# Four result tiles in place of two, and the last sequence's averaging products ahead of an output product

## The chip, the cores and the metric

The kernel runs on one core of one Trainium2 chip. The metric is device time in microseconds (us) of one execution; lower is better. Names of engines: PE is TensorE (PEld its weight loads), DVE is VectorE, ACT is ScalarE, POOL is GpSimd, SP is SyncE, which here only issues DMAs.

## The reference

A block over eight sequences of 512 rows and 128 channels, all in float32. After a layer norm, one branch is a recurrent attention (a running weighted mean over time), the other is one expert of a feed-forward layer with a second layer norm and a SiLU; their product is added to the input.

```python
xn = layernorm(x)                                   # x: (8, 512, 128)
shifted = pad(xn, one row of zeros ahead)[:, :-1]
k, v, r = (mix(xn, shifted, m) @ W for m, W in ((mk, Wk), (mv, Wv), (mr, Wr)))
wkv = scan over t of (e1 * num + e2 * v) / (e1 * den + e2)
s = (sigmoid(r) * wkv) @ Wo
z = xn + relu(xn @ w1 + b1) @ w2 + b2               # expert 0 alone has a weight, 1
g = silu((z - mean(z)) * rsqrt(var(z) + 1e-5) * gamma + beta)
out = x + s * g
```

## The kernel before

Each sequence is one tile of 128 channels (partitions) by 512 time steps, so a step of the work on one sequence is mostly one instruction. The order of the work is written out by hand: `PROGRAM` (line 27) holds one list of steps for each engine, and `run` (line 280) issues them. A token `s:5` is step `s` of sequence 5; `var.a:7` is the first half (256 time steps) of step `var` of sequence 7. Only the first and the last sequence have halves. Each engine takes its list strictly in its order, and waits at a step for all that the step names by `after`.

The last part of the program is what matters here. For one sequence it goes like this:

- `gated` (DVE, line 849) is the gated attention result, in `gated[b % 2]`. It reads the bank of `r`, which is free after it.
- `s` (PE, line 661) is the output product with `Wo`, into a bank. A float32 product of 512 columns is two matmuls in the trace.
- `sq` (ACT, line 523) squares z; `var` (PE, line 668) is the averaging product: it multiplies the squares by a matrix of 1/128, which gives the variance of each column. `ln_var` and `rstd2` (ACT, lines 529 and 536) make the inverse root of it from a logarithm and an exponential, `zn` (DVE, line 858) the normed z, and `silu` (ACT, line 584) the gate g. Between `rstd2` and `silu` stands a load of another activation table (line 455), between `sq` and `ln_var` one too (line 452).
- `prod` (DVE, line 866) multiplies g with the bank of `s`; `back` (PE, line 689) transposes it to rows, four matmuls of 128 columns; `res` (DVE, line 875) adds the input and writes the result tile `res[b % 2]`; `store` (line 307) sends the tile out, 256 KB, from SP's queue. The last half, `res.b:7`, goes out from ACT's queue (line 593).

Two kinds of resource tie the steps together besides the data:

- Eight PSUM banks. `BANKS` (line 78) lists for each bank who holds it in turn, and `FREED_BY` (line 90) which step frees it. `bank_free` (line 247) makes a PE step wait for that. The bank of `var.a:7` was held by `r:6`, so the step waits for `gated:6`; the bank of `var.b:7` was held by `v:7`, so it waits for `wkv:7`; that of `s:5` was held by `k:7`, so it waits for `adev:7`.
- Result tiles. `res` of sequence b writes a tile that the store of sequence b - 2 reads, so `add_input` (line 868) waits until that store has landed (`stored`, two semaphores).

`prod:5` waits for `s:5`, and `gated:7` reuses the tile of `gated:5`, which `s:5` reads.

Of the kernel before, what the change touches and what calls it, by code (L numbers as in the profile page):

```python
# [7 lines left out]
ALU = mybir.AluOpType  # L8
# [4 lines left out]
WARM_UP = 8  # L13
KEEP_WARM_BETWEEN = 1
KEEP_WARM = 4
LN_EXP_TABLES = "natural_log_exp_and_others"
SILU_TABLES = "silu_and_others"

# [13 lines left out]
        up1:3 k:3 z2:3 z0:3 z1:3 var:2 s:0 z3:3 up3:4 k:4 T:5 up0:4 up2:4 var:3 s:1 back:0 v:3 up1:4  # L32
        back:1 z3:4 z0:4 v:4 s:2 up2:5 z1:4 z2:4 r:3 T:6 up1:5 r:4 z2:5 k:5 var:4 up3:5 up0:5 T:7
        up1:6 v:5 up0:6 up2:6 s:3 up3:6 r:5 k:6 z1:5 z0:5 z3:5 k:7 z3:6 var:5 z1:6 z0:6 z2:6 v:6
        back:2 var:6 up1:7 up2:7 up3:7 v:7 s:4 z2:7 up0:7 r:6 r:7 z1:7 z3:7 z0:7 back:3 s:5 var.b:7
        var.a:7 back:4 s:6 s.b:7 back:5 s.a:7 back:6 back.a:7 back.b:7
    """,
    "act": """
        ln_exp ve.a:0 rs.a:0 neg_td ve.b:0 rs.b:0 w1_hi xT.a:0 xT.b:0 wo ve:1 rs:1 hid0:0 xT:1
# [7 lines left out]
        ln_var:4 hid3:5 rstd2:4 xT:7 hid0:5 e_new:5 e_keep:5 hid0:6 v_sb:5 hid2:6 ln_den:5 silu_set  # L47
        th_g:5 silu:4 hid3:6 th_r:5 th_a:5 sq:5 ln_exp e_new:6 e_keep:6 ln_var:5 rstd2:5 e_keep:7
        sq:6 ln_den:6 e_new:7 v_sb:6 ln_var:6 rstd2:6 ln_den:7 hid2:7 silu_set th_g:6 v_sb:7 th_a:6
        th_g:7 silu:5 hid0:7 th_a:7 th_r:7 silu:6 th_r:6 sq.a:7 sq.b:7 ln_exp ln_var.b:7 ln_var.a:7  # L50
        rstd2.b:7 rstd2.a:7 silu_set silu.a:7 silu.b:7
    """,
    "dve": """
        bn.a:0 aggr1.a:0 bn.b:0 aggr1.b:0 norm1.a:0 norm1.b:0 cols bn:1 aggr1:1 d:0 w2_sum inv:0
# [5 lines left out]
        dev:4 gated:3 adev:4 wkv:4 mx:5 gated:4 gap:5 inv:6 zn:4 hid1:6 ink:6 den:5 prod:3 inr:6  # L60
        rel:5 ink:7 mx:6 dev:5 gap:6 adev:5 mx:7 gap:7 wkv:5 den:6 gated:5 zn:5 inv:7 res:2 den:7
        hid1:7 rel:6 inr:7 zn:6 rel:7 prod:4 hid3:7 dev:6 adev:6 dev:7 wkv:6 adev:7 wkv:7 gated:6
        res:3 prod:5 gated:7 res:4 zn.b:7 zn.a:7 prod:6 res:5 prod.a:7 prod.b:7 res:6 res.a:7
        res.b:7
    """,
    "pool": """
# [62 lines left out]
def build_block(nc, x, vectors, squares, w1, w2, out):  # L129
    B, T, H = x.shape  # L130
    P = 128
    NT = T // P
# [5 lines left out]
    out_rows = out.rearrange("b (j p) c -> b p j c", p=P)  # L138
# [8 lines left out]
    with ExitStack() as ctx:  # L147
        def sb(name, *shape, dt=FP32):
            return ctx.enter_context(nc.sbuf_tensor(name, list(shape), dt))

        def pair(name, *shape, dt=FP32):
            return [sb(f"{name}_{n}", *shape, dt=dt) for n in range(2)]
# [25 lines left out]
        ve1 = sb("ve1", P, B * NT)  # L178
        rstd1 = sb("rstd1", P, B * NT)
        xn = pair("xn", P, NT, P)  # L180
        res = pair("res", P, NT, P)


        xT = pair("xT", P, 1 + T)
# [12 lines left out]
        th_g = pair("th_g", P, T)  # L197
# [6 lines left out]
        gated = pair("gated", P, T)  # L204
        hid = pair("hid", P, NF, T)
        sq = pair("sq", P, T)
        ln_var = pair("ln_var", P, T)
        rstd2 = pair("rstd2", P, T)
        zn = pair("zn", P, T)
        g = pair("g", P, T)  # L210
        prod = pair("prod", P, T)
# [3 lines left out]
        def ps(name, b, half=""):  # L215
            return banks[bank_of[name, half if (name, half, b) in bank_of else "", b]]

        def sem(name):
            return ctx.enter_context(nc.semaphore(name))
# [5 lines left out]
                 "w2_sum", "w2_mean", "w2"]}  # L225
        done = {(engine, name): sem(f"{name}_by_{engine}")
                for engine, name in dict.fromkeys((signal[token][0], token[0]) for token in signal if token[2] is not None)}
        stored = [sem(f"stored_{n}") for n in range(2)]
        EDGES = 11
        LAST = B - 1  # L230
        CHUNKS = [f"z{f}" for f in range(NF)]

        def after(eng, step, b, half=""):
            if b < 0 or (b == 0 and step in NOT_FOR_FIRST):
                return
            if (step, half, b) in signal:
                engine, count = signal[step, half, b]
            elif half:
                engine, count = signal[step, "", b]
            else:  # L240
                engine, count = max(signal[step, h, b] for h in "ab")
            eng.wait_ge(done[engine, step], count)
# [13 lines left out]
        def chunks_of(b):  # L256

            return [name for name, _, i in tokens("pe") if name in CHUNKS and i == b]
# [4 lines left out]
        def tiles(half):  # L263
            return {"": slice(0, NT), "a": HALVES[0], "b": HALVES[1]}[half]
# [8 lines left out]
        def first_on(engine, step):  # L273
            return [b for name, _, b in tokens(engine) if name == step][0]
# [23 lines left out]
        def load_half(eng, h):  # L298
            tiles = HALVES[h]
            eng.dma_start(x_sb[:, tiles.start * P:tiles.stop * P].rearrange("p (j c) -> p j c", c=P),  # L300
                          x_rows[0][:, tiles, :]).then_inc(got[f"x0_{h}"], 16)

        def load(eng, b):
            eng.dma_start(x_sb[:, b * T:(b + 1) * T].rearrange("p (j c) -> p j c", c=P),
                          x_rows[b]).then_inc(got[f"x{b}"], 16)

        def store(eng, b, half=""):
            after(eng, "res", b, half)
            eng.dma_start(out_rows[b][:, tiles(half), :], res[b % 2][:, tiles(half), :]).then_inc(stored[b % 2], 16)

        block = ctx.enter_context(nc.Block())

        @block.sync
        def _(sp):
            load_half(sp, 0)
            sp.dma_start(w1_in[:, :], w1).then_inc(got["w1"], 16)
            sp.dma_start(w_in[:, :, :], squares).then_inc(got["squares"], 16)
            load(sp, 1)
            sp.dma_start(w2_in[:, :, :], w2.rearrange("(f p) c -> p f c", p=P)).then_inc(got["w2"], 16)
            for b in range(2, B):  # L320
                load(sp, b)
            for b in range(LAST):
                store(sp, b)
            store(sp, LAST, "a")
            sp.wait_ge(stored[0], 16 * (B // 2))
            sp.wait_ge(stored[1], 16 * (B // 2 + 1))

        @block.gpsimd
        def _(pool):
# [117 lines left out]
        def _(act):  # L447
# [3 lines left out]
            def ln_exp_tables():  # L451
                act.preload_act_table_set(LN_EXP_TABLES)  # L452

# [137 lines left out]
            steps.update({f"hid{f}": hidden(f) for f in range(NF)})  # L591
            run("act", steps)
            store(act, LAST, "b")

        @block.tensor
        def _(pe):
            def keep_warm(count):
                for _ in range(count):
                    pe.matmul(banks[WARM_BANK][:, 0:P], ident[:, :], ident[:, :], start=True, stop=True)  # L599
# [8 lines left out]
            def transposes(b, half=""):  # L608
# [9 lines left out]
                elif b == 0:  # L618
                    keep_warm(KEEP_WARM)

# [80 lines left out]
        def _(dve):  # L701
# [166 lines left out]
            def add_input(b, half=""):  # L868
                t = tiles(half)
                after(dve, "back", b, half)  # L870
                if b >= 2:
                    dve.wait_ge(stored[b % 2], 16 * (b // 2))
                rows = x_sb[:, b * T:(b + 1) * T].rearrange("p (j c) -> p j c", c=P)
                summed = ps("back", b, half)[:, :].rearrange("p (j c) -> p j c", c=P)
                dve.tensor_tensor(res[b % 2][:, t, :], summed[:, t, :], rows[:, t, :], ALU.add).then_inc(done["dve", "res"], 1)

            steps = {"bn": stats, "aggr1": aggregate, "norm1": normalise, "d": step_of_x, "xT_lo": low_part, "dv": value_steps,
                     "cols": small_columns, "w2_sum": w2_row_sums, "mx": running_max, "gap": exponents,
                     "den": denominator, "rel": relative, "dev": deviation,
                     "wkv": mixed_values, "gated": gate, "zn": scale, "prod": multiply, "res": add_input,  # L880
                     "adev": weighted}
            steps.update({"in" + name: mix(name) for name in "kvr"})
# [35 lines left out]
```

## Time and profile before

| What | Value |
|---|---|
| Time, median of 3 runs | 111.28 us (110.7 to 111.68) |
| Time of the profiled execution | 111.6 us |
| Its span (first to last instruction) | 109.8 us |
| PE busy | 100.7 us, 92% |
| DVE busy | 99.3 us, 90% |
| ACT busy | 93.4 us, 85% |
| POOL busy | 67.0 us, 61% |
| DMA | 5.09 MB, mean 46 GB/s |

The span is a part of the time: the profiled execution has 1.8 us around it. Times inside the span count from its start. Busy shares are means over the whole span; they don't say which engine sets the end. In a row of the timeline, two numbers stand first: the start, and the length in us. Rows of a merged group (x2, x4) give the whole group's length. The records of matmuls overlap, since they are pipelined, so their cadence is read from the starts.

### The profile page before, as it was taken

The numbers are of one execution on the slowest core, as the hardware profiler recorded it, in microseconds if no ns is written. First come the engines' busy times: TensorE is split into PE (matmuls) and PEld (weight loads), VectorE is DVE, ScalarE is ACT, GpSimd is POOL, SyncE is SP. The second block draws the span as 40 slices with busy tenths as digits, with TensorE's granted clock in tenths as the row PEclk, the third lists the DMA queues.
The fourth block names the chain that finished last, engine by engine and source line by source line (L and its number), as shares of the span: only waits on it lengthen the run. The fifth ranks groups of instructions, "written<-read, shape, count | busy, mean of one in ns | idle before, by whom it ended". The sixth has DMA issues, their size and how long they took to land.

```text
span 109.8 us, 1625 instructions
## 1 busy us (share of the span) xinstructions
PE 100.7 (92%) x340; PEld 57.8 (53%) x340; DVE 99.3 (90%) x204; ACT 93.4 (85%) x155; POOL 67.0 (61%) x102
## 2 busy tenths in 40 slices
PE   4999989999699999999999999999989999999720
PEld 4998546654346465436574554754424565435410
DVE  1789799999889999998999899999999999999941
ACT  3550888999979999999999999999998999998800
POOL 3059699986838599999699669594645033700000
PEclk9999999999999999999999999999999999999995
DMA  2999300000000000000005000000000020001463
GB/s 90 279 314 291 83 0 0 0 6 0 3 0 3 0 0 0 0 0 0 0 15 178 1 6 0 0 0 3 0 0 0 0 96 0 9 0 57 134 191 99
DMA packets 9450, 5.09 MB, mean 46 GB/s; under 512 B 480, under 2 KB 9184, under 8 KB 9440
## 3 DMA queue, kind: packets, MB, share of 16 engines
q1 hardware_dynamic: 8752, 4.72, 15.3%
q10 hardware_dynamic: 688, 0.27, 0.9%
q14 instruction: 7, 0.06, 0.2%
q8 instruction: 3, 0.05, 0.2%
HBM read 2.89 MB, written 2.10 MB: 45 GB/s over the span
## 4 chain that ended last, share of the span: by engine, by line
PE 56%; issue 15%; POOL 13%; ACT 6%; DVE 5%; DMA 2%; DVEq 1%; POOLq 0%; ACTq 0%
PE bank L630 11%; PE bank L680 10%; PE bank L599 5%; PE bank L661 5%; PE bank L668 5%; PE bank L651 4%; POOL xn L359 4%; PE bank L653 4%; PE bank L652 4%; PE bank L613 3%; PE bank L643 3%; POOL xT_lo L381 2%; DMA block_out<-res 2%; POOL gap_max L415 2%; PE bank L689 2%
## 5 line engine op out<-in xcount | busy, mean ns | idle before, releaser
L680 PE MATMUL bank<-hid,w_c 128*128 128x512 f32 x64 | 30.8, 593 | 0.3 <-ACT hid L514 0.3
L630 PE MATMUL bank<-mixed,w_in 128*128 128x512 f32 x48 | 24.0, 599 | 1.1 <-POOL mixed L399 1.1
L514 ACT ACTIVATE hid<-bank,vec 128x512 f32<-128x512 f32 x28 | 18.8, 684 | 3.6 <-PE bank L643 2.9
L680 PEld LDWEIGHTS bank<-hid,w_c 128*128 128x128 f32 x64 | 11.9, 189 | 12.6 <-issue 11.6
L786 DVE SCALAR_TENSOR_TENSOR mixed<-step_x,vec,bank 128x511 f32<-128x511 f32 x24 | 17.2, 735 | 0.8 <-POOL step_x L390 0.8
L651 PE MATMUL bank<-xT_hi,w_hi 128*128 128x512 f32 x28 | 15.7, 560 | 0.0
L359 POOL TENSOR_SCALAR xn<-x_sb,neg_mean,rstd 128x128 f32<-128x128 f32 x28 | 14.1, 521 | 0.1
L630 PEld LDWEIGHTS bank<-mixed,w_in 128*128 128x128 f32 x48 | 8.4, 189 | 9.3 <-issue 8.2
L423 POOL TENSOR_TENSOR dv<-v_sb 128x512 f32<-128x512 f32 x8 | 8.9, 1108 | 6.1 <-ACT v_sb L567 6.1
L825 DVE TENSOR_TENSOR_SCAN dev<-keep,dv 128x512 f32<-128x512 f32 x8 | 11.5, 1435 | 0.6 <-issue 0.3
L653 PE MATMUL bank<-xT_lo,w_hi 128*128 128x512 f32 x28 | 11.1, 395 | 0.0
L652 PE MATMUL bank<-xT_hi,w_lo 128*128 128x512 f32 x28 | 11.0, 394 | 0.0
L795 DVE TENSOR_TENSOR_SCAN mx<-td,bank 128x512 f32<-128x512 f32 x8 | 9.7, 1210 | 0.7 <-PE bank L630 0.7
L430 POOL TENSOR_SCALAR keep<-th_g 128x512 f32<-128x512 f32 x8 | 5.8, 723 | 6.3 <-ACT th_g L573 6.2
L810 DVE TENSOR_TENSOR_SCAN den<-e_keep,bank 128x512 f32<-128x512 f32 x8 | 9.6, 1208 | 0.0
L452 ACT ACT_TABLE_LOAD x6 | 7.7, 1283 | 1.9 <-issue 1.8
L710 DVE BATCH_NORM_STATS2 stats<-x_sb 128x6 f32<-128x128 f32 x32 | 6.9, 278 | 2.6 <-DMA x_sb<-x 2.6
L381 POOL TENSOR_TENSOR xT_lo<-xT,xT_hi 128x512 fp32r<-128x512 f32 x7 | 8.9, 1267 | 0.3
L668 PE MATMUL bank<-sq,averager 128*128 128x512 f32 (+1 forms) x18 | 8.3, 557 | 0.5 <-DVE adev L833 0.5
L661 PE MATMUL bank<-gated,wo_half 128*128 128x512 f32 (+1 forms) x18 | 8.3, 553 | 0.0
L651 PEld LDWEIGHTS bank<-xT_hi,w_hi 128*128 128x128 f32 x28 | 5.3, 188 | 5.5 <-issue 2.1
L407 POOL TENSOR_SCALAR gap_min<-gap,td 128x512 f32<-128x512 f32 x8 | 5.5, 688 | 4.2 <-DVE gap L803 4.0
(72 smaller groups left out, 209.9 us busy)
## 6 DMA issues: line engine op xcount, KB each, us to landing
x_sb<-x SPq DMA_DIRECT2D x7, 256.0 KB, 5.4
block_out<-res SPq DMA_DIRECT2D x7, 256.0 KB, 2.3
w_in<-w SPq DMA_DIRECT2D x2, 256.0 KB, 4.0
w_in<-squares SPq DMA_DIRECT2D x1, 256.0 KB, 3.9
x_sb<-x ACTq DMA_DIRECT2D x1, 128.0 KB, 2.8
x_sb<-x SPq DMA_DIRECT2D x1, 128.0 KB, 2.5
block_out<-res SPq DMA_DIRECT2D x1, 128.0 KB, 1.9
block_out<-res ACTq DMA_DIRECT2D x1, 128.0 KB, 2.0
```

What stands on the lines that cost most here:

```text
L359: ins = pool.tensor_scalar(xn[n][:, j, :], x_tile(b, j), neg_mean1[:, i:i + 1], rstd1[:, i:i + 1], ALU.add, ALU.mult)
L381: pool.tensor_tensor(xT_lo[n][:, :], xT[n][:, 1:], xT_hi[n][:, :].bitcast(FP32), ALU.subtract).then_inc(done["pool", "xT_lo"], 1)
L514: act.activation(hid[b % 2][:, f, :], ps(f"up{f}", b)[:, :], ACT.Relu, bias=vec[:, B1_COLUMN + f:B1_COLUMN + f + 1]).then_inc(done["act", ...
L630: pe.matmul(ps(name, b)[:, :], w_in[:, which, :], mixed[b % 2][:, which, :], start=True, stop=True).then_inc(done["pe", name], 1)
L651: pe.matmul(dst, hi, xT_hi[n][:, :], start=True, stop=False)
L652: pe.matmul(dst, lo, xT_hi[n][:, :], start=False, stop=False)
L653: pe.matmul(dst, hi, xT_lo[n][:, :], start=False, stop=True).then_inc(done["pe", f"up{f}"], 1)
L661: pe.matmul(ps("s", b, half)[:, c], wo_half[:, :], gated[b % 2][:, c], start=True, stop=True).then_inc(done["pe", "s"], 1)
L668: pe.matmul(ps("var", b, half)[:, c], averager[:, :], sq[b % 2][:, c], start=True, stop=True).then_inc(done["pe", "var"], 1)
L680: pe.matmul(ps("z", b)[:, :], w2_c[:, f, :], hid[b % 2][:, f, :], start=False, stop=chunks_of(b)[-1] == f"z{f}", skip_group_check=True).th ...
L786: dve.scalar_tensor_tensor(mixed[n][:, which, 1:], step_x[n][:, 1:], vec[:, which:which + 1], ps("z", b)[:, 0:T - 1], ALU.mult, ALU.add).t ...
L825: dve.tensor_tensor_scan(dev[n][:, :], keep[n][:, 0:T], dv[n][:, :], 0.0, ALU.mult, ALU.add).then_inc(done["dve", "dev"], 1)
```

## The change

`res` has four tiles in place of two, and there are four `stored` semaphores. So `res` of sequence b waits for the store of sequence b - 4, and `res:0` to `res:3` wait for none. In the program of PE, the averaging products of sequence 7 stand ahead of `s:5` in place of behind it, and half a ahead of half b. ACT's `ln_var` and `rstd2` and DVE's `zn` of sequence 7 also take half a first. `BANKS` and `FREED_BY` stay as they are. All else stays.

```diff
@@ PROGRAM "pe"
-        back:2 var:6 up1:7 up2:7 up3:7 v:7 s:4 z2:7 up0:7 r:6 r:7 z1:7 z3:7 z0:7 back:3 s:5 var.b:7
-        var.a:7 back:4 s:6 s.b:7 back:5 s.a:7 back:6 back.a:7 back.b:7
+        back:2 var:6 up1:7 up2:7 up3:7 v:7 s:4 z2:7 up0:7 r:6 r:7 z1:7 z3:7 z0:7 back:3 var.a:7
+        var.b:7 s:5 back:4 s:6 s.b:7 back:5 s.a:7 back:6 back.a:7 back.b:7
@@ PROGRAM "act"
-        th_g:7 silu:5 hid0:7 th_a:7 th_r:7 silu:6 th_r:6 sq.a:7 sq.b:7 ln_exp ln_var.b:7 ln_var.a:7
-        rstd2.b:7 rstd2.a:7 silu_set silu.a:7 silu.b:7
+        th_g:7 silu:5 hid0:7 th_a:7 th_r:7 silu:6 th_r:6 sq.a:7 sq.b:7 ln_exp ln_var.a:7 ln_var.b:7
+        rstd2.a:7 rstd2.b:7 silu_set silu.a:7 silu.b:7
@@ PROGRAM "dve"
-        res:3 prod:5 gated:7 res:4 zn.b:7 zn.a:7 prod:6 res:5 prod.a:7 prod.b:7 res:6 res.a:7
+        res:3 prod:5 gated:7 res:4 zn.a:7 zn.b:7 prod:6 res:5 prod.a:7 prod.b:7 res:6 res.a:7
@@ tiles and semaphores
+RES = 4
-        res = pair("res", P, NT, P)
+        res = [sb(f"res_{n}", P, NT, P) for n in range(RES)]
-        stored = [sem(f"stored_{n}") for n in range(2)]
+        stored = [sem(f"stored_{n}") for n in range(RES)]
@@ store
-            eng.dma_start(out_rows[b][:, tiles(half), :], res[b % 2][:, tiles(half), :]).then_inc(stored[b % 2], 16)
+            eng.dma_start(out_rows[b][:, tiles(half), :], res[b % RES][:, tiles(half), :]).then_inc(stored[b % RES], 16)
@@ the end of SP's program
-            sp.wait_ge(stored[0], 16 * (B // 2))
-            sp.wait_ge(stored[1], 16 * (B // 2 + 1))
+            for n in range(RES):
+                sp.wait_ge(stored[n], 16 * (B // RES + (n == LAST % RES)))
@@ add_input
-                if b >= 2:
-                    dve.wait_ge(stored[b % 2], 16 * (b // 2))
+                if b >= RES:
+                    dve.wait_ge(stored[b % RES], 16 * (b // RES))
-                dve.tensor_tensor(res[b % 2][:, t, :], summed[:, t, :], rows[:, t, :], ALU.add).then_inc(done["dve", "res"], 1)
+                dve.tensor_tensor(res[b % RES][:, t, :], summed[:, t, :], rows[:, t, :], ALU.add).then_inc(done["dve", "res"], 1)
```

On PE, near the end, the order before was this. The rows are, in turn, the last matmul of `back:3`, then `s:5`, `var.b:7`, `var.a:7`, `back:4`, `s:6` and `s.b:7`, each with the semaphores it waits for:

```order
L689 MATMUL bank<-ident,prod 128x128 x3
L661 MATMUL bank<-gated,wo_half 128x512 [waits adev_by_dve,gated_by_dve]
L668 MATMUL bank<-sq,averager 128x256 [waits wkv_by_dve,v_sb_by_act,sq_by_act]
L668 MATMUL bank<-sq,averager 128x256 [waits gated_by_dve,sq_by_act]
L689 MATMUL bank<-ident,prod 128x128 [waits hid0_by_act,prod_by_dve]
L689 MATMUL bank<-ident,prod 128x128 x3
L661 MATMUL bank<-gated,wo_half 128x512 [waits res_by_dve,gated_by_dve]
L661 MATMUL bank<-gated,wo_half 128x256 [waits gated_by_dve]
```

And now, where every line number is one higher:

```order
L690 MATMUL bank<-ident,prod 128x128 x3
L669 MATMUL bank<-sq,averager 128x256 [waits gated_by_dve,sq_by_act]
L669 MATMUL bank<-sq,averager 128x256 [waits wkv_by_dve,v_sb_by_act,sq_by_act]
L662 MATMUL bank<-gated,wo_half 128x512 [waits adev_by_dve,gated_by_dve]
L690 MATMUL bank<-ident,prod 128x128 [waits hid0_by_act,prod_by_dve]
L690 MATMUL bank<-ident,prod 128x128 x3
L662 MATMUL bank<-gated,wo_half 128x512 [waits res_by_dve,gated_by_dve]
L662 MATMUL bank<-gated,wo_half 128x256 [waits gated_by_dve]
```

The step that waits for `gated` (of sequence 6, for its bank) now stands first of the three, and `s:5`, which waited only for `adev:7` and `gated:5`, stands behind both averaging products.

On DVE, at the very end, the order before was, from `prod:5` on:

```order
L866 TENSOR_TENSOR prod<-bank,g 128x512 [waits back_by_pe,s_by_pe,silu_by_act]
L849 SCALAR_TENSOR_TENSOR gated<-bank,wkv 128x512 [waits s_by_pe,th_r_by_act,wkv_by_dve]
L875 TENSOR_TENSOR res<-bank,x_sb 128x512 [waits stored_0,back_by_pe]
L858 SCALAR_TENSOR_TENSOR zn<-bank,cb,rstd_1 128x256 [waits silu_by_act,rstd2_by_act,sq_by_act] x2
L866 TENSOR_TENSOR prod<-bank,g 128x512 [waits back_by_pe,s_by_pe,silu_by_act]
L875 TENSOR_TENSOR res<-bank,x_sb 128x512 [waits stored_1,back_by_pe]
L866 TENSOR_TENSOR prod<-bank,g 128x256 [waits back_by_pe,s_by_pe,silu_by_act] x2
L875 TENSOR_TENSOR res<-bank,x_sb 128x512 [waits stored_0,back_by_pe]
L875 TENSOR_TENSOR res<-bank,x_sb 128x256 [waits stored_1,back_by_pe] x2
```

And now:

```order
L867 TENSOR_TENSOR prod<-bank,g 128x512 [waits back_by_pe,s_by_pe,silu_by_act]
L850 SCALAR_TENSOR_TENSOR gated<-bank,wkv 128x512 [waits s_by_pe,th_r_by_act,wkv_by_dve]
L876 TENSOR_TENSOR res<-bank,x_sb 128x512 [waits stored_0,back_by_pe]
L859 SCALAR_TENSOR_TENSOR zn<-bank,cb,rstd_1 128x256 [waits silu_by_act,rstd2_by_act,sq_by_act] x2
L867 TENSOR_TENSOR prod<-bank,g 128x512 [waits back_by_pe,s_by_pe,silu_by_act]
L876 TENSOR_TENSOR res<-bank,x_sb 128x512 [waits stored_1,back_by_pe]
L867 TENSOR_TENSOR prod<-bank,g 128x256 [waits back_by_pe,s_by_pe,silu_by_act] x2
L876 TENSOR_TENSOR res<-bank,x_sb 128x512 [waits stored_2,back_by_pe]
L876 TENSOR_TENSOR res<-bank,x_sb 128x256 [waits stored_3,back_by_pe] x2
```

The order of DVE's steps is the same but for the halves of `zn`; what moved is the semaphore of the last two rows. Before, `res.a:7` waited for three stores on `stored_1`, the last of them that of `res:5`; now it waits for one on `stored_3`, that of `res:3`.

## Rows read from the trace of the kernel before

**Rows 1.** The page, busy time of each engine, and PE and DVE in 40 slices

```profile
PE 100.7 (92%) x340; PEld 57.8 (53%) x340; DVE 99.3 (90%) x204; ACT 93.4 (85%) x155; POOL 67.0 (61%) x102
...
DVE  1789799999889999998999899999999999999941
```

**Rows 2.** Timeline of DVE, 98 to 108 us: start, length, line, operation, idle before

```profile
98.15 0.69 DVE L841 SCALAR_TENSOR_TENSOR wkv<-adev,bank 128x512 f32<-128x512 f32 x1
98.75 0.68 DVE L849 SCALAR_TENSOR_TENSOR gated<-bank,wkv 128x512 f32<-128x512 f32 x1
99.36 0.68 DVE L875 TENSOR_TENSOR res<-bank,x_sb 128x512 f32<-128x512 f32 x1
99.95 0.68 DVE L866 TENSOR_TENSOR prod<-bank,g 128x512 f32<-128x512 f32 x1
...
101.75 0.86 DVE L858 SCALAR_TENSOR_TENSOR zn<-bank,cb,rstd 128x256 f32<-128x256 f32 x2
...
103.13 0.68 DVE L875 TENSOR_TENSOR res<-bank,x_sb 128x512 f32<-128x512 f32 x1
103.72 0.74 DVE L866 TENSOR_TENSOR prod<-bank,g 128x256 f32<-128x256 f32 x2
104.39 0.68 DVE L875 TENSOR_TENSOR res<-bank,x_sb 128x512 f32<-128x512 f32 x1
106.58 0.75 DVE L875 TENSOR_TENSOR res<-bank,x_sb 128x256 f32<-128x256 f32 x2 [1.52 <-DMA block_out<-res]
```

**Rows 3.** The chain that ended last, 103 to 106 us: start, length, what

```profile
103.83 2.29 DMA block_out<-res
```

**Rows 4.** Timeline of PE and its weight loads, 97 to 105 us

```profile
97.60 0.63 PE L689 MATMUL bank<-ident,prod 128*128 128x128 f32 x4 [0.22 <-DVE wkv L841]
98.20 1.10 PE L661 MATMUL bank<-gated,wo_half 128*128 128x512 f32 x2
98.95 0.19 PEld L668 LDWEIGHTS bank<-sq,averager 128*128 128x128 f32 x1 [0.48 <-issue]
99.14 1.12 PE L668 MATMUL bank<-sq,averager 128*128 128x256 f32 x4
99.55 0.19 PEld L668 LDWEIGHTS bank<-sq,averager 128*128 128x128 f32 x1 [0.22 <-issue]
99.58 0.45 PE L668 MATMUL bank<-sq,averager 128*128 128x256 f32 x1
100.09 0.60 PE L689 MATMUL bank<-ident,prod 128*128 128x128 f32 x4
100.53 1.02 PE L661 MATMUL bank<-gated,wo_half 128*128 128x512 f32 x2
...
104.28 0.74 PE L689 MATMUL bank<-ident,prod 128*128 128x128 f32 x4 [0.30 <-DVE prod L866]
```

**Rows 5.** Timeline of ACT, 99 to 104 us

```profile
99.77 0.99 ACT L529 ACTIVATE ln_var<-bank,eps 128x256 f32<-128x256 f32 x2 [0.21 <-PE bank L668]
...
101.39 1.28 ACT L455 ACT_TABLE_LOAD   x1
102.69 1.09 ACT L584 ACTIVATE g<-zn,vec 128x256 f32<-128x256 f32 x2
```

**Rows 6.** Stretches of 0.2 us: engines' busy times, granted clock, DMA share, GB/s

```profile
106.00:106.20 0.20, 0.00 (x0) 0.00 (x0) 0.00 (x0) 0.00 (x0) 0.00 (x0) 1.00 0.83 256
...
106.60:106.80 0.20, 0.00 (x0) 0.00 (x0) 0.20 (x1) 0.00 (x0) 0.00 (x0) 0.56 0.95 287
...
107.80:108.00 0.20, 0.00 (x0) 0.00 (x0) 0.00 (x0) 0.00 (x0) 0.00 (x0) 0.50 0.20 64
...
108.80:109.00 0.20, 0.00 (x0) 0.00 (x0) 0.00 (x0) 0.00 (x0) 0.00 (x0) 0.50 0.34 92
```

**Rows 7.** Timeline of the queues: issues of the last two stores on SP

```profile
105.09 0.37 SPq L309 DMA_DIRECT2D block_out<-res  x1
...
107.03 0.37 SPq L309 DMA_DIRECT2D block_out<-res  x1
```

## The prediction

> **What bounds the kernel now.** I read the busy shares first [rows 1]. PE and DVE are both busy for nine tenths of the span, so no share names the bound; DVE's line of slices stands at 8 or 9 from slice 6 to slice 38, and then falls to 4. So the end is a stage of its own, and the change touches only that stage. I then read DVE's timeline over the last 12 us [rows 2]. From `wkv:7` at 98.15 to the end of `res:6` at 105.07 no row has an idle time: one instruction of 512 columns starts every 0.60 us, and that cadence, not the recorded length of 0.68, is what a step costs. The two halves `res.a:7` and `res.b:7` start at 106.58, after 1.52 us of idle time that is put down to a store. The chain of waits names which [rows 3]: the store issued at 103.83, when `res:5` ended (103.13 + 0.68 = 103.81), took 2.29 us to land. So in the last stage DVE sets the pace up to 105.07, then a store that holds a result tile, then two halves and their own stores.
>
> Next PE, since three of its steps trade places [rows 4]. `back:3` ends near 98.2; `s:5` starts at 98.20 and its second matmul ends at 99.30. The weight load of `var.b:7` starts at 98.95 after 0.48 us without a load, 0.11 after `wkv:7` ended (98.15 + 0.69 = 98.84), and its matmuls follow from 99.14. The weight load of `var.a:7` starts at 99.55, 0.12 after `gated:6` ended (98.75 + 0.68 = 99.43). Both averaging products thus wait for their banks already, and the rows put it down to "issue", which hides it. Before, `s:5` runs in the time of the first wait.
>
> **The result tiles.** With four tiles, `res.a:7` waits for the store of `res:3`, whose row in DVE's timeline starts at 99.36 [rows 2]: by the 2.29 us of [rows 3] it lands near 102.3. The wait is gone. What is late next is DVE itself: the slot behind `res:6` is 104.39 + 0.60 = 104.99, and `back.b:7` ends at 104.28 + 0.74 = 105.02 [rows 4], in time for the second half. Alone, this part lets `res.a:7` start 106.58 - 104.99 = 1.59 us sooner. Earlier `res` steps had no wait, so the two more tiles give nothing there. The two further waits at the end of SP's program are for stores that have landed; I count them at nothing, since the last store covers them.
>
> **The order on PE.** Now `var.a:7` stands first, and it can't load its weights before 99.55, since `gated:6` isn't moved. Behind it are queued `var.b:7`, `s:5`, `back:4` and all that follows. No row shows `s:5` there, but one shows the same pattern: in before, `var.a:7` starts at 99.58, the next step at 100.09, the one behind that, `s:6`, at 100.53 and ends at 100.53 + 1.02 = 101.55 [rows 4]. After: `var.a:7` at 99.58, `var.b:7` at 100.09 (two matmuls with 0.21 to 0.22 between starts, as 99.14 to 99.58 shows for two), `s:5` at about 100.53, its end at 101.55. The wait of `prod:5` on it ends at 101.60, 0.05 later (ACT started `ln_var` 0.04 after the end of its matmul in before, 99.77 in [rows 5]). `prod:5` began at 99.95, so DVE loses 101.60 - 99.95 = **1.65 us**, in one idle stretch in front of `prod:5`. Behind `prod:5` wait `gated:7`, `res:4` and the whole tail of DVE, and since DVE had no idle time there, nothing takes up the loss: `res:6` starts at 104.39 + 1.65 = 106.04.
>
> The bounds of this: if the bank wait weren't there, PE could start at 98.23 behind `back:3`, `s:5` would come 0.88 later (four matmuls at 0.22), end at 100.2, and DVE would lose 0.25 us; the lower end is 0.25. With the wait for `wkv:7` alone (load at 98.95) it would lose about 1.0. The upper end is that the matmuls behind the hole run at half speed (below): 3.6. I take 1.65, since the row of `gated:6` gives it directly.
>
> **The order of the halves.** ACT's first logarithm started at 99.77, with 0.21 us of waiting for PE [rows 5]. Now its input is `var.a:7`, whose second matmul ends at about 100.25, so ACT's tail comes 0.5 later: table load at 101.9 (was 101.39), `silu.a:7` ready to run at 103.2 (was 102.69). DVE's tail is 1.65 later, so this is hidden: the first half of `zn` comes at 101.75 + 1.65 = 103.4 [rows 2], `silu.a:7` at 104.0, its end at 104.6, and `prod.a:7` is due at 103.72 + 1.65 = 105.37. If the cover were gone it would cost at most the 0.5. PE's later steps (`s.b:7`, `back:5`, `s.a:7`, `back:6`) each wait for a DVE step that is 1.65 later and keep their distance to the next.
>
> **The sum on DVE.** `res.a:7` starts at 106.04 + 0.60 = 106.64, against 106.58: 1.65 - 1.59 = +0.06. The stall has moved from behind `res:6` to in front of `prod:5`.
>
> **The stores.** In before the data of `res:6` began to move at 106.0, and those of the two halves together moved from 107.95 to 108.87 (shares of 0.20 and 0.34 in the two outer stretches) [rows 6]. Those of `res:6` begin 0.92 after its issue at 105.09, those of the halves 0.92 after 107.03 [rows 7]; 256 KB take 0.90 at 290 GB/s. After: `res:6` ends at 106.72, its data start at 106.74 + 0.92 = 107.66. The halves are issued at 107.1 (SP is busy with the issue before it until then, 0.37) and, from ACT, at 107.4, behind `res.b:7`, and their data would start at 108.0, while the engines are busy to 108.56. So 512 KB go from 107.66 without a gap, 1.81 us, to 109.47, against 108.87: **+0.60**, and this contains the 0.06. The ends: if the transfers didn't add up, the last one would end 0.06 later than in before; if each had to land before the next, `res:6` at 106.74 + 2.29 = 109.03 and a half about 1 us behind it, 110.0 to 110.5 for the last data, +1.1 to +1.6. I take 0.60, since the engines' share is at 0.83 to 0.95 during a single 256 KB store [rows 6] and leaves no room for a second.
>
> The Trainium skill, page "DMA: Bandwidth & Descriptors", section "Issuing engines are not separate DMA queues", says that transfers issued by ScalarE and SyncE run on the same 16 DMA engines and interleave; by that rule the half from ACT's queue isn't spared, and the sum stays at +0.60, where a separate path would give +0.06 to +0.3. The stretches agree in that the share is near full during one store; no row of before shows two full stores overlapping.
>
> **The time.** The profiled execution took 111.6 us with a span of 109.8. With +0.60 it is 112.2. It stands 0.32 above the median of the runs, 111.28, so the prediction is 111.28 + 0.60 = **111.9 us**. A measurement of this kernel tells about 1% (1.1 us) from no change, and this is half of it: no change that can be told, leaning to slower.
>
> **The rivals.**
>
> *The stall is small.* If `s:5` were late by only the 0.25 us of the lower end, the tiles' gain would stay: `res:6` is issued at 105.34, data from 106.26, the end of 512 KB at 108.07, -0.8; with no delay at all -1.06. That gives 110.2 to 110.5 us. For it: the rows name "issue", not a semaphore, before both weight loads. Against it: the loads start 0.11 and 0.12 after the two DVE steps that free the banks, and the order shows `gated_by_dve` in front.
>
> *Slower: the clock falls in PE's new hole.* PE ends `back:3` near 98.23 and starts again at 99.58: 1.35 us without a matmul. In before, PE's last matmul ends at 105.02, and the granted clock falls in the stretch 106.60 to 106.80 (0.56) to 0.50, so from 2.4 to 1.2 GHz, 1.6 us later [rows 4, 6]. It decides if the fall comes before PE is busy again. Price: from 99.58 to the end of `s:5`, 1.97 us of matmuls take twice that, so `prod:5` starts 1.97 later than in the forecast: 111.9 + 2.0 = 113.9, and more if PE stays slow behind it. Against it: the hole is shorter than those 1.6 us, and before it PE is busy without a break, where the last transposes of before already had idle time ahead of them (0.30 us at 104.28). The Trainium skill, page "TensorE: Matmul & The Clock Gate", section "What's actually happening", has the clock at full speed after sustained work and at half after idling; which side a hole like this one falls on, no run here shows yet.
>
> *Slower: the stores bunch up worse than their bytes.* The last three stores are issued within 0.7 us. If they are served one after the other with their landing in between, the end comes 1.1 to 1.6 later: 112.4 to 112.9. Against it: the data of two halves ran without a gap in before.
>
> *The change doesn't do what it says.* `res.a:7` could still wait, now for `stored_3`. That store lands 4 us earlier; I leave 1 in 100.
>
> **How the numbers follow.** Forecast 0.68 (own range 111.3 to 112.5), small stall 0.13 (110.2 to 110.5, with the spread of a median a part of it goes below 110.17), clock 0.07, bunched stores 0.11, no effect of the tiles 0.01. Faster by over 1% (under 110.17): 0.09. Slower by over 1% (over 112.39): clock 0.07, bunched stores 0.09, and 0.05 from the forecast's upper edge, 0.21. Within 1%: 0.70. The range of 110.5 to 113.0 leaves out the clock case and most of the small-stall case below.
>
> **What would show it.** In the changed kernel: DVE's row of `prod:5` near 101.6 with about 1.6 us idle before it, released by PE's output product; `res.a:7` directly behind `res:6` with no idle time, near 106.6; PE idle from 98.2 to 99.6 with its averaging weights loaded at 99.55; ACT's first logarithm near 100.3; a granted clock of 1.00 at 100 us; DMA busy from 107.7 to 109.5 without a gap; a span near 110.4. An idle time before `prod:5` under 1 us, or a `res.a:7` before 106, would make the forecast wrong; so would a clock of 0.50 before 105.

## The result, and the profile after

| | Before | After |
|---|---|---|
| Time, median | 111.31 us (6 runs) | 112.55 us (6 runs, 112.03 to 112.88) |
| Time of the profiled execution | 111.6 us | 112.88 us |
| Its span | 109.8 us | 111.1 us |

The ratio is 1.0105, with a 95% interval of 1.0076 to 1.0134: slower by 1.2 us. The forecast was 111.9 us and no change that can be told. The range of 110.5 to 113.0 holds the result, but the change is just past the 1% that I took as the line, on the side to which the forecast leaned; its interval lies on both sides of that line.

DVE's timeline of the changed kernel, beside [rows 2], and its only wait in the last 11 us:

```profile
98.75 0.68 DVE L850 SCALAR_TENSOR_TENSOR gated<-bank,wkv 128x512 f32<-128x512 f32 x1
99.35 0.68 DVE L876 TENSOR_TENSOR res<-bank,x_sb 128x512 f32<-128x512 f32 x1
101.63 0.69 DVE L867 TENSOR_TENSOR prod<-bank,g 128x512 f32<-128x512 f32 x1 [1.60 <-issue]
...
105.42 0.75 DVE L867 TENSOR_TENSOR prod<-bank,g 128x256 f32<-128x256 f32 x2
106.08 1.35 DVE L876 TENSOR_TENSOR res<-bank,x_sb 128x512 f32<-128x512 f32 x3
```

```profile
DVE prod L867 <- issue: 1.6, 1, 1.6
```

The idle time of 1.52 us ahead of `res.a:7` is gone, and one of 1.60 us stands ahead of `prod:5`. The row of `res` now groups three instructions, `res:6`, `res.a:7` and `res.b:7`, without a gap, and ends at 107.43; before, the halves ended at 106.58 + 0.75 = 107.33. "issue" as releaser hides who was waited for. PE's timeline, beside [rows 4], tells it:

```profile
97.60 0.63 PE L690 MATMUL bank<-ident,prod 128*128 128x128 f32 x4 [0.20 <-DVE wkv L842]
99.58 1.10 PE L669 MATMUL bank<-sq,averager 128*128 128x256 f32 x4 [1.35 <-DVE gated L850]
100.52 1.02 PE L662 MATMUL bank<-gated,wo_half 128*128 128x512 f32 x2
...
105.98 0.74 PE L690 MATMUL bank<-ident,prod 128*128 128x128 f32 x4 [0.30 <-DVE prod L867]
```

Here the releaser is named: the first of the averaging products, `var.a:7`, waited 1.35 us for `gated:6`, which frees its bank. The output product `s:5` stands behind them, ends at 101.54, and `prod:5` starts at 101.63. ACT's first logarithm, beside [rows 5], came at 100.29, and its silu waited 0.85 us for `zn`, so the order of the halves was hidden:

```profile
100.29 0.90 ACT L530 ACTIVATE ln_var<-bank,eps 128x256 f32<-128x256 f32 x2 [0.71 <-PE bank L669]
...
103.95 1.09 ACT L585 ACTIVATE g<-zn,vec 128x256 f32<-128x256 f32 x2 [0.85 <-DVE zn L859]
```

Up to DVE's last instruction the changed kernel is only 0.10 us later than the kernel before. The rest of the 1.3 us in the span comes behind it. Stretches of 0.2 us, beside [rows 6] (behind the engines' busy times: granted clock, the mean busy share of the core's 16 DMA engines, GB/s):

```profile
107.60:107.80 0.20, 0.00 (x0) 0.00 (x0) 0.00 (x0) 0.00 (x0) 0.00 (x0) 1.00 0.30 92
...
108.60:108.80 0.20, 0.00 (x0) 0.00 (x0) 0.00 (x0) 0.00 (x0) 0.00 (x0) 0.74 0.94 277
...
109.20:109.40 0.20, 0.00 (x0) 0.00 (x0) 0.00 (x0) 0.00 (x0) 0.00 (x0) 0.50 0.92 297
109.40:109.60 0.20, 0.00 (x0) 0.00 (x0) 0.00 (x0) 0.00 (x0) 0.00 (x0) 0.50 0.69 208
109.60:109.80 0.20, 0.00 (x0) 0.00 (x0) 0.00 (x0) 0.00 (x0) 0.00 (x0) 0.50 0.08 23
109.80:110.00 0.20, 0.00 (x0) 0.00 (x0) 0.00 (x0) 0.00 (x0) 0.00 (x0) 0.50 0.08 23
```

The burst of 512 KB begins at 107.7 and nearly all of it has moved by 109.55, as the sum of bytes said (109.47). But then a share of 0.08, that is little more than one engine of the 16, goes on until 110.1. One DMA engine lagged by half a microsecond, and the run can't end before it. (No view names the engine; that it is one is read from the share.)

The DMA traffic just ahead of the burst, by queues (the share of 16 engines stands last):

```profile
q14 instruction: 1, 0.01, 16.6%
q1 hardware_dynamic: 10, 0.00, 3.4%
```

This is the changed kernel from 107.4 to 107.7: between two bursts of stores (q1, the queue of SP's stores; q10 is that of ACT's) one packet of 8 KB for instructions (q14). Its record begins at 107.53 and takes 0.80 us (16.6% of 16 engines in 0.3 us), so it reaches 0.6 us into the last burst. In the kernel before, such a packet came at 107.24 and took 0.45 us, in a gap between stores that ended at 107.92. Its row in the stretch from 107.2 to 107.3:

```profile
q14 instruction: 1, 0.01, 27.9%
```

### The profile page after: what moved, and what is told of

It reads as the page before. It is cut to its first block and busy times, and to the rows that moved or that the text cites. A ratio compares the mean times of both kernels' runs of the same rounds, so it can differ in the third digit from the quotient of the medians.

```text
span 111.1 us, 1624 instructions
## 1 busy us (share of the span) xinstructions
PE 100.5 (91%) x340; PEld 57.3 (52%) x340; DVE 99.3 (89%) x204; ACT 93.3 (84%) x155; POOL 66.8 (60%) x102
```

## The experiments

Since the start of a run shifts the whole stage by up to 0.7 us between profiles, the table counts each from the start of `gated:6`. "DVE" is from there to the end of DVE's last instruction, "stores" from there to the last store packet (read to 0.05 us from fine stretches), "rest" from that packet to the end of the span. The ratio is to the kernel before, with its 95% interval.

| Kernel | DVE | stores | rest | Ratio |
|---|---|---|---|---|
| before | 8.58 | 1.64 | 0.80 | 1 |
| the changed kernel | 8.68 | 2.67 | 0.95 | 1.0105 (1.0076 to 1.0134) |
| e1_tiles_only | 6.97 | 2.53 | 0.95 | 0.9952 (0.9931 to 0.9974) |
| e2_order_only | 10.28 | 1.62 | 0.80 | 1.0159 (1.0129 to 1.0188) |
| e3_free_bank | 7.64 | 2.54 | 0.95 | 1.0006 (0.9981 to 1.0030) |
| e4_product_first | 7.17 | 2.34 | 0.80 | 0.9938 (0.9916 to 0.9961) |
| e5_stores_apart | 7.78 | 2.05 | 0.85 | 0.9986 (0.9959 to 1.0013) |
| e6_changed_stores_apart | 9.16 | 2.01 | 0.85 | 1.0117 (1.0079 to 1.0154) |
| e7_b_first | 8.24 | 2.53 | 0.95 | 1.0076 (1.0045 to 1.0108) |
| e8_three_tiles | 6.97 | 2.46 | 0.75 | 0.9923 (0.9895 to 0.9951) |
| e9_vector_ends_last | 8.67 | 2.47 | 1.00 | 1.0117 (1.0083 to 1.0152) |
| e10_changed_three_tiles | 8.67 | 2.45 | 0.75 | 1.0088 (1.0053 to 1.0124) |
| e11_one_queue | 8.67 | 2.53 | 0.80 | 1.0106 (1.0072 to 1.0139) |
| e12_padded | 8.67 | 2.23 | 0.80 | 1.0058 (1.0035 to 1.0081) |

### The two parts of the change by themselves

**e1_tiles_only**: the kernel before with `RES = 4` and all that goes with it; the programs of the engines as before.

> The kernel before with four result tiles and nothing else changed. Theory (the tiles take 1.59 us out, the order on TensorE puts 1.65 us in, and stores at the end add up by their bytes): the stall ahead of res.a:7 is gone, res.a:7 starts at 105.0 in place of 106.58, there is no stall ahead of prod:5, and the data of the last three stores go without a gap from 106.0 to 107.8, 1.1 us earlier than before (108.95). Time against the kernel before -0.9 to -1.1 us, ratio 0.990 to 0.992. If in addition one DMA engine lags as in the changed kernel, only -0.4 to -0.6, ratio 0.995. Rival (the tiles themselves cost, by the two further semaphores or by stores that bunch up, and the order costs little): ratio 1.000 or above.

DVE's last rows of e1:

```profile
103.63 0.74 DVE L867 TENSOR_TENSOR prod<-bank,g 128x256 f32<-128x256 f32 x2
104.29 1.34 DVE L876 TENSOR_TENSOR res<-bank,x_sb 128x512 f32<-128x512 f32 x3
```

No wait is left, and DVE ends 1.61 us earlier (6.97 against 8.58), as the prediction's sum had it (1.59). But the time fell by only 0.5%, 0.5 us. The stores behind DVE's end take 2.53 us in place of 1.64, and the rest behind the last packet 0.15 more: of 1.61 us, 1.04 is given back there. The expectation's second number, the one with a lagging engine, is what came.

**e2_order_only**: the kernel before, two tiles, with the change's lines of `PROGRAM`.

```diff
-        ... back:3 s:5 var.b:7
-        var.a:7 back:4 s:6 s.b:7 back:5 s.a:7 back:6 back.a:7 back.b:7
+        ... back:3 var.a:7
+        var.b:7 s:5 back:4 s:6 s.b:7 back:5 s.a:7 back:6 back.a:7 back.b:7
```

> The kernel before with the new order of the averaging products (and of the halves on the other engines), and two result tiles as before. Theory: prod:5 starts at 101.6 after 1.6 us of idle time; res:5 ends near 105.5, its store lands 2.3 us later, near 107.8, and res.a:7 starts near 108.2, 1.65 us later than before; the stores then have the spacing of before. Time +1.65 us, ratio 1.015. Rival (the order is cheap and the loss of the changed kernel comes from its stores): res.a:7 within 0.5 us of before, ratio below 1.005.

```profile
101.03 0.69 DVE L866 TENSOR_TENSOR prod<-bank,g 128x512 f32<-128x512 f32 x1 [1.60 <-issue]
...
107.66 0.76 DVE L875 TENSOR_TENSOR res<-bank,x_sb 128x256 f32<-128x256 f32 x2 [1.51 <-DMA block_out<-res]
```

Both idle times are there, 1.60 and 1.51 us, in series. DVE ends 1.70 us later, the stores keep their 1.62, and the ratio is 1.0159, 1.8 us. The two parts add: +1.59% and -0.48% make +1.11%, against +1.05% for both together. So the order costs three times what the tiles give.

### What the stall is

**e3_free_bank**: the changed kernel, with `var.a:7` in a bank that is free since `adev:6`.

```diff
-... s:3 k:6
+... s:3 k:6 var.a:7
-... s:4 r:6 var.a:7 back:5
+... s:4 r:6 back:5
```

> The changed kernel with one edit: var.a:7 writes into bank 4, free since adev:6 near 96, in place of bank 3, which gated:6 frees at 99.43. Theory (the hole on TensorE is the wait for that bank): var.a:7 starts right behind back:3 at 98.2, var.b:7 at 98.98 (it still waits for wkv:7), s:5 near 99.4 and ends near 100.45, prod:5 starts near 100.5 with 0.5 us of idle time in place of 1.6. res.a:7 comes 1.1 us earlier than in the changed kernel. Ratio to the kernel before 1.000 to 1.002, against 1.0105 for the changed kernel. Rival (the averaging products are late for another reason, their squares or the table load, or the loss is in the stores): the idle time ahead of prod:5 stays at 1.6 and the ratio at 1.010.

PE and DVE of e3:

```profile
97.64 0.60 PE L669 MATMUL bank<-sq,averager 128*128 128x256 f32 x2
98.55 0.67 PE L669 MATMUL bank<-sq,averager 128*128 128x256 f32 x2 [0.32 <-DVE wkv L842]
99.06 1.02 PE L662 MATMUL bank<-gated,wo_half 128*128 128x512 f32 x2
...
100.17 0.69 DVE L867 TENSOR_TENSOR prod<-bank,g 128x512 f32<-128x512 f32 x1 [0.57 <-issue]
```

`var.a:7` no longer waits for `gated`; `var.b:7` waits 0.32 us for `wkv:7`, and the idle time ahead of `prod:5` is 0.57 in place of 1.60. Ratio 1.0006 in place of 1.0105, from one name in the table of banks. This shows that the bank, not the place in the list alone, makes the order dear.

**e7_b_first**: the changed kernel with half b ahead of half a on PE, ACT and DVE, `s:5` still behind both.

```diff
-        ... back:3 var.a:7
-        var.b:7 s:5 back:4
+        ... back:3 var.b:7
+        var.a:7 s:5 back:4
```

> The changed kernel with half b ahead of half a again on all engines; s:5 stays behind both averaging products. Theory (the matmul queued first waits for its bank, and half b's is free 0.6 us earlier): var.b:7 starts at 98.98, var.a:7 at 99.58, s:5 at 100.05 and ends near 101.1, so the idle time ahead of prod:5 is 1.1 to 1.2 us in place of 1.60, and the ratio to before is 1.006 to 1.007 against 1.0105. Rival (the order of the halves is of no account, the place of s:5 is all): idle time 1.6, ratio 1.010.

```profile
99.01 1.27 PE L669 MATMUL bank<-sq,averager 128*128 128x256 f32 x4 [0.75 <-DVE wkv L842]
...
101.24 0.69 DVE L867 TENSOR_TENSOR prod<-bank,g 128x512 f32<-128x512 f32 x1 [1.17 <-issue]
```

Close to what was expected: PE starts 0.57 us earlier, the stall is 1.17, and the ratio 1.0076, a little above the 1.006 to 1.007.

**e4_product_first**: the changed kernel with `s:5` first, half a still ahead of half b.

```diff
-        ... back:3 var.a:7
-        var.b:7 s:5 back:4
+        ... back:3 s:5 var.a:7
+        var.b:7 back:4
```

> The changed kernel with s:5 back ahead of both averaging products; half a still goes ahead of half b, and there are four tiles. Theory (all of the stall comes from s:5 being queued behind the bank wait, and the order of the halves is nearly hidden): no idle time ahead of prod:5; ScalarE starts its first logarithm at 100.3 (0.5 later than before), its last silu ends near 104.2, and prod.b:7 is up to 0.2 us late. Ratio to before 0.991 to 0.994, and within 0.002 of the kernel with the tiles alone. Rival (the order of the halves costs its full 0.5 us): 0.005 slower than the kernel with the tiles alone.

```profile
99.29 1.10 PE L669 MATMUL bank<-sq,averager 128*128 128x256 f32 x4 [0.28 <-DVE gated L850]
...
103.46 0.91 DVE L867 TENSOR_TENSOR prod<-bank,g 128x256 f32<-128x256 f32 x2
```

No stall ahead of `prod:5`. PE's wait for the bank is still there, but 0.28 us long and with nothing due behind it. The two halves of `prod` take 0.91 us as a group in place of 0.74, which is the 0.2 us that the order of the halves costs once its cover is gone (DVE 7.17 against 6.97 of e1). By time, e4 and e1 can't be told apart (0.9938 and 0.9952, intervals that overlap). The stall thus has four sizes in four kernels, 1.60, 1.17, 0.57 and 0, with ratios 1.0105, 1.0076, 1.0006 and 0.9938.

### Where the stores' time goes

**e5_stores_apart** and **e6_changed_stores_apart**: e4 and the changed kernel, each with `prod:6` ahead of the halves of `zn` and `res:6` ahead of `prod.a:7` on DVE.

```diff
-        res:3 prod:5 gated:7 res:4 zn.a:7 zn.b:7 prod:6 res:5 prod.a:7 prod.b:7 res:6 res.a:7
+        res:3 prod:5 gated:7 res:4 prod:6 zn.a:7 zn.b:7 res:5 res:6 prod.a:7 prod.b:7 res.a:7
```

> The kernel e4_product_first with one edit on VectorE: prod:6 goes ahead of the two halves of zn:7, and res:6 ahead of prod.a:7 and prod.b:7, so that the store of res:6 is issued 0.7 us earlier while res.b:7 comes about 0.3 later (it waits for the transposes of the halves). Theory (the end is set by 512 KB of stores in one burst, which the 8 KB fetch of instructions at the end of VectorE's work makes longer by one lagging DMA engine): the burst splits, the last one has 256 KB and takes 1.0 us as in the kernel before, the last packet comes 0.4 to 0.5 us earlier than in e4. Ratio to before 0.989 to 0.991. Rival (the end is set by VectorE's last instruction plus a fixed time of a store): 0.3 us slower than e4, ratio 0.996.

> The changed kernel with the same edit on VectorE as e5_stores_apart: prod:6 and res:6 earlier. The stall of 1.6 us ahead of prod:5 stays. Theory (0.6 us by the bytes and 0.5 us by the lagging engine were lost in the stores of the changed kernel): the last packet comes 0.5 to 0.9 us earlier than in the changed kernel, ratio to before 1.003 to 1.006. Rival (the stores cost nothing beyond VectorE's end): ratio 1.011 to 1.014.

Both missed. e5 is slower than e4 (0.9986 against 0.9938), e6 not faster than the changed kernel (1.0117 against 1.0105). DVE's rows of e5 say one half of it:

```profile
102.08 0.69 DVE L867 TENSOR_TENSOR prod<-bank,g 128x512 f32<-128x512 f32 x1 [0.22 <-PE bank L662]
...
105.68 0.86 DVE L876 TENSOR_TENSOR res<-bank,x_sb 128x256 f32<-128x256 f32 x2 [0.26 <-PE bank L690]
```

DVE waits twice, and with a longer last pair it ends 0.61 us later than in e4. The other half: the burst didn't split. The stores of `res:5` and `res:6` now lie back to back and the halves follow without a gap, 768 KB from 105.09 to 108.56, so the stores behind DVE's end fell only from 2.34 to 2.05. e6 has the same form: DVE ends 0.48 us later than in the changed kernel, and the stores behind it take 0.66 less. In both, the fetch came inside the burst (at 107.18 and 108.08), and about one engine's share was still busy in the last 0.5 us. My theory that the burst would split, and with it the lag go, falls. So does e5's rival of an end at DVE plus a fixed time, since the stores behind DVE's end changed.

**e11_one_queue**: the changed kernel with `store(sp, LAST, "b")` on SP in place of ACT.

> The changed kernel with the last half's store issued by SP, behind that of res.a:7, in place of ScalarE. Theory (bytes and the fetch set the end, not the queues): the burst keeps its 2.2 to 2.4 us and the ratio its 1.010 to 1.012, at most 0.1 us more for the later issue. Rival (packets of two queues on one lagging engine cost each other): the burst shrinks to 1.9 us and the ratio to 1.007.

The burst took 2.23 us and the ratio is 1.0106: the lag is there with a single queue too, so two queues on the lagging engine aren't its cause. They do go with the longer "rest" of the table. In the five profiles where it is 0.95 or more, the last packets of q1 and q10 end 0.03 us apart, both in the tail of the burst. In the other nine it is 0.75 to 0.85 (0.80 in e11), and the last packets of the two queues end 0.29 us or more apart, or there is one queue. The times of e11 and the changed kernel don't tell the 0.15 us apart.

**e9_vector_ends_last**: the changed kernel, and at the end of DVE's program

```diff
             run("dve", steps)
+            dve.wait_ge(stored[LAST % RES], 16 * (B // RES + 1))
```

> The changed kernel; VectorE's program gets one wait at its very end, for the last store to land, so that VectorE runs out of its program only after all stores. Theory (the 8 KB fetch of instructions comes when VectorE runs out of its program, lands on one DMA engine in the middle of the last stores, and that engine then lags by 0.4 to 0.6 us): the fetch moves behind the last store, and the last burst of 512 KB takes 1.8 to 1.9 us in place of 2.38. If nothing new shows at the end, the ratio to before is 1.006; if the fetch is then itself at the end, it eats the gain, 1.010 to 1.014. Rival (the lag is in the stores themselves, from two queues on one engine or from 512 KB in one burst): the burst still takes 2.2 us or more. Rival (the fetch belongs to another engine): it stays near VectorE's last instruction.

The fetch stayed, at 107.65 (DVE ended at 107.55), the burst took 2.20 us, and the ratio is 1.0117. So the fetch isn't caused by DVE running out of its program; this part of the theory falls. Left open was a fetch that an engine asks for at a place in its program.

**e12_padded**: the changed kernel with 16 small instructions more.

```diff
         def _(dve):
+            for n in range(16):
+                dve.memset(pad[:, n:n + 1], 0.0)
```

> The changed kernel with 16 more one-column memsets into a scratch tile at the start of VectorE's program, where it waits for data anyway. Theory (the last 8 KB fetch of instructions is VectorE's, asked for when it reaches a certain place in its program, and the lag of one DMA engine comes from it): the fetch comes 16 instructions earlier, near 98 us, away from the last stores; the last burst of 512 KB takes 1.9 to 2.0 us in place of 2.2 to 2.4; ratio to before 1.007. Rival (the fetch belongs to another engine or to the end of the run): it stays beside the last burst, the burst keeps its 2.2 to 2.4 us, ratio 1.0105. Rival (the lag isn't the fetch's): the fetch moves, and the burst stays at 2.2 to 2.4 us.

Sixteen instructions more went with a lower time: 111.76 us, ratio 1.0058 in place of 1.0105. The intervals overlap by a little (1.0035 to 1.0081 and 1.0076 to 1.0134), but the profiles tell the same, and e9 and e11, which end as the changed kernel does, stand at 1.0117 and 1.0106. DMA of e12 from 103.0 to 103.7, where nothing is stored:

```profile
DMA packets 1, 0.01 MB, mean 12 GB/s; under 512 B 0, under 2 KB 0, under 8 KB 0
## 3 DMA queue, kind: packets, MB, share of 16 engines
q14 instruction: 1, 0.01, 4.6%
```

and its last stretches:

```profile
107.60:107.80 0.20, 0.00 (x0) 0.00 (x0) 0.00 (x0) 0.00 (x0) 0.00 (x0) 1.00 0.74 225
...
109.20:109.40 0.20, 0.00 (x0) 0.00 (x0) 0.00 (x0) 0.00 (x0) 0.00 (x0) 1.00 0.96 289
109.40:109.60 0.20, 0.00 (x0) 0.00 (x0) 0.00 (x0) 0.00 (x0) 0.00 (x0) 1.00 0.36 98
109.60:109.80 0.20, 0.00 (x0) 0.00 (x0) 0.00 (x0) 0.00 (x0) 0.00 (x0) 1.00 0.00 0
```

The fetch has moved from 107.53 to 103.08. The burst of 512 KB takes 1.96 us in place of 2.38 and ends with all engines together; no tail at a share of 0.08 is left. Stores behind DVE's end: 2.23 in place of 2.67. The edit touches nothing but DVE's program and a scratch tile of 16 columns, so the fetch is tied to a place in that program; that it came 4.5 us earlier and not the 9.5 that I had expected (near 98) shows that I can't place it exactly. Of the five fetches on q14 behind 30 us, two moved: this one, and one from 59.97 to 52.62. The other three stayed within 0.1 us, so they seem to belong to other engines' programs.

The price of the fetch isn't the same in all profiles. The packets' records of the kernels that end in one burst of 512 KB give:

| Kernels | Fetch ends after the burst began by | Burst, us |
|---|---|---|
| e12 | no fetch there | 1.96 |
| e8, e10 | 0.19, 0.20 us | 2.16, 2.17 |
| e4 | 0.35 us | 2.05 |
| e1, e3, e7, e9, e11 | 0.45 to 0.49 us | 2.20 to 2.24 |
| the changed kernel | 0.63 us | 2.38 |

All nine bursts with a fetch are longer than the one without, by 0.09 to 0.42 us, and the one that the fetch reached furthest into is the longest; e4 is out of order, so there is no fixed price for an overlap. The changed kernel's profile has the highest price of the nine. e9, e10 and e11, where DVE takes the same 8.67 us, have 2.17 to 2.23, that is 0.21 to 0.27 us. The burst without a fetch is a single profile. The Trainium skill, page "Runtime: NRT & Kernel Launch", section "Instruction fetch mechanics", says that each engine's sequencer drives its own DMA queue to fetch the next block of its program while it works on the current one, and calls the cost mostly hidden. This trace agrees in that the fetch follows VectorE's program. It doesn't show a queue for each engine: q14 carried two fetches that moved with VectorE's program and three that didn't. And the cost isn't hidden where the fetch meets the last stores (2.38 us against 1.96).

### The number of tiles

**e8_three_tiles** and **e10_changed_three_tiles**: e1 and the changed kernel with three tiles.

```diff
-RES = 4
+RES = 3
-                sp.wait_ge(stored[n], 16 * (B // RES + (n == LAST % RES)))
+                sp.wait_ge(stored[n], 16 * (len(range(n, B, RES)) + (n == LAST % RES)))
```

> The kernel e1_tiles_only with three result tiles in place of four. Theory (res.a:7 then waits for the store of res:4, which lands near 104.1, before it is due at 105.0): the same as with four, ratio to before 0.995. Rival (the wait is for more than that one store): res.a:7 is late, ratio up to 1.000.

> The changed kernel with three result tiles in place of four. If the 0.3 us between three and four tiles (0.9923 against 0.9952, in different sets of runs) belongs to the number of tiles or semaphores: ratio to before 1.0075. If it is scatter: 1.0105, as the changed kernel. In both, 1.6 us of idle time ahead of prod:5 and none ahead of res.a:7.

Three tiles free `res.a:7` as four do: DVE takes the same 6.97 and 8.67. e8 has a median of 110.26 us, the lowest of all. Like e1 and e4 it beats both kernels, by 0.8% (before) and 1.8% (changed); from e1 and e4 it can't be told apart. Both kernels with three tiles have a lower ratio than their partners with four, by 0.003 and 0.002, and 0.75 us of rest in place of 0.95. But the intervals overlap in both pairs, and the shorter rest goes with the queues' last packets ending 0.39 us apart (see e11), as in kernels with four tiles and a rest of 0.80. So whether the third of a microsecond belongs to the number of tiles stays open.

## Why the prediction was right or wrong

- *The wait of `res.a:7` goes, worth 1.59 us on DVE.* Right: 1.61 in e1. It isn't worth that in time, since the stores then bunch up; the prediction said so (-1.06 with no stall), and e1 gave -0.5.
- *`prod:5` comes 1.65 us later, since `s:5` is queued behind the wait for `gated:6`'s bank.* Right, 1.68 (101.63 against 99.95), 1.60 of it idle. The row of `s:6` behind `back:4` as a pattern gave the start to 0.01: `s:5` forecast at 100.53 and found at 100.52. e3, e4 and e7 vary the cause and the stall follows.
- *The order of the halves is hidden.* Right: silu waited 0.85 us for `zn`. Without the cover it costs 0.2 on DVE (e4), where the bound was 0.5.
- *The sum on DVE, +0.06.* Right: +0.10.
- *The stores, +0.60, which contains the 0.06.* This term was mis-sized. From DVE's end to the last packet, 0.54 was forecast and 1.03 measured. The bytes' part held: with the fetch out of the way (e12) the stores take 2.23 - 1.64 = 0.59 longer than before. The missing 0.44 is one DMA engine that lags beside an instruction fetch of 8 KB; that a fetch could meet the burst was not in the sum. The page of the profile before lists queue q14 with its 7 packets, and a fetch stood at 107.24, 0.68 ahead of the last burst; in the changed kernel it comes 0.17 ahead. Another 0.15 is between the last packet and the end of the span, where the sum had nothing; in the profiles it goes with the two queues' last packets ending together (e11). The prediction also read the end of a burst too early (108.87 in the kernel before, where the last packet ends at 108.97; 1.81 us for 512 KB, where e12 has 1.96). It did so on both sides, so nearly all of it cancels in the difference.
- *Rival, small stall:* fell; 1.60 us.
- *Rival, the clock falls in PE's hole:* fell. The granted clock stays at 1.00 through the 1.35 us without a matmul and up to 108.7.
- *Rival, the stores bunch up worse than their bytes:* its price came true (+1.1 to +1.6; measured +1.13 to the last packet and +1.28 in the span), and so did its 112.4 to 112.9 us, where 112.55 lies. Its mechanism, stores that wait for each other's landing, didn't: the data moved without a gap.
- *No effect of the tiles:* fell.

So the mechanism of the stall and of the tiles was right, and one term was too small by half a microsecond. The result lies just outside the forecast's own 111.3 to 112.5. That it lies inside 110.5 to 113.0 is in part luck: that range was wide enough for a rival whose mechanism didn't happen. The chances of 0.70 for a change within 1% and 0.21 for slower by more rested on the term of the stores; with the 0.44 the forecast would have stood at 112.3, at the edge of the two.

## What to carry to other kernels

Before a step is moved ahead on an in-order engine, list every semaphore it waits for, the one that frees its output buffer too: the step then holds up all that is queued behind it, and moving its buffer may be worth more than moving the step. An earlier end of compute is worth only what the final stores let through, so add up the bytes of the stores that come to lie together, and look at what else their DMA engines do then, instruction fetches included. Where a profile puts a wait down to "issue", look at what another engine ended just before: here such rows were waits for a step that had ended 0.1 us earlier (101.54 and 101.63).

## What the runs showed of the hardware

- One fetch of 8 KB of instructions beside the start of a burst of stores held up one DMA engine, and with it the end, by 0.1 to 0.4 us: the burst of 512 KB took 2.05 to 2.38 us in nine kernels with the fetch at its start and 1.96 without, in one profile of the padded kernel. The record of the fetch took 0.80 us in the changed kernel and 0.45 in the kernel before.
- Two of the five fetches on queue q14 behind 30 us moved with 16 more instructions in DVE's program (107.53 to 103.08, 59.97 to 52.62), and three did not.
- 512 KB of stores moved at 241 to 312 GB/s in the full stretches of 0.2 us (107.8 to 109.4), with a share of 0.87 to 1.01 of the 16 engines; 256 KB alone took 1.05 us from first to last packet (107.92 to 108.97 in the kernel before).
- The granted clock fell 1.6 us after the last matmul in the kernel before and 2.0 us after it in the changed kernel (106.72 to 108.7), and in e12 it was still at 1.00 more than 3 us after it (last matmul at 106.64, clock 1.00 at 109.8). A hole of 1.35 us left it at 2.4 GHz.
